# Transposing attention probabilities four heads at a time, and multiplying by values in 64x64 tiles

## The reference

```
x = x + xattn(layernorm(x), ctx_1024, ...)
x = x + ffn(layernorm(x), w_gate, w_up, w_down)

def xattn(x, context, ...):
    q = (layernorm(x) @ w_q).reshape(B, SQ, 16, 64)
    k, v = split(context @ w_kv)                    # 77 keys, 16 heads of 64
    attn = softmax(einsum("bqhd,bkhd->bhqk", q * SCALE, k))
    out = einsum("bhqk,bkhd->bqhd", attn, v).reshape(B, SQ, 1024)
    return (out @ w_out + b_out) * tanh(gate[0])

def ffn(x, w_gate, w_up, w_down):                   # integer weights times 1/127
    return (silu(x @ wg.T) * (x @ wu.T)) @ wd.T
```

## Time and profile before

| | |
|---|---|
| median of 3 runs | 308.63 us |
| the profiled execution | 308.18 us |
| its span, first to last instruction | 305.8 us |
| PE busy | 292.3 us (96%) |
| DVE, ACT, POOL busy | 233.1, 170.4, 165.8 us |
| granted TensorE clock, mean | 0.998 |

### The profile page before, as it was taken

One profiled execution on the slowest core, in us unless ns is written; L12 is line 12 of the kernel. 1 busy time (PEld: TensorE's weight loads), 2 busy tenths in 40 slices (PEclk: granted clock), 3 DMA queues, 4 the chain that ended last, 5 costly groups with the idle time before them and its releaser, 6 DMA issues.

```text
span 305.8 us, 6324 instructions
## 1 busy us (share of the span) xinstructions
PE 292.3 (96%) x2351; PEld 269.6 (88%) x2351; DVE 233.1 (76%) x610; ACT 170.4 (56%) x326; POOL 165.8 (54%) x164
## 2 busy tenths in 40 slices
PE   6899999997989999999999999999999999999985
PEld 6898978786888899889998989898989898988984
DVE  2298897686789788878887797779777878786773
ACT  4456884667328734772496249525943694167052
POOL 3381863357857680857095629553863487227033
PEclk9999999999999999999999999999999999999999
DMA  7994154412423021002201020202020201110001
GB/s 203 376 368 115 38 172 180 173 62 103 147 74 102 0 78 58 13 13 67 69 2 47 31 69 2 76 2 69 3 77 2 69 2 41 34 38 0 2 30 40
DMA packets 16313, 23.27 MB, mean 76 GB/s; under 512 B 1634, under 2 KB 13898, under 8 KB 16282
## 3 DMA queue, kind: packets, MB, share of 16 engines
q1 hardware_dynamic: 16282, 22.85, 22.8%
HBM read 15.87 MB, written 4.62 MB: 67 GB/s over the span
## 4 chain that ended last, share of the span: by engine, by line
PE 86%; DVE 5%; POOL 3%; ACT 2%; issue 2%; DMA 1%; DVEq 0%; POOLq 0%; ACTq 0%; SPq 0%
PE ps L822 13%; PE ps L768 9%; PE ps L754 8%; PE ps L728 6%; PE ps L736 5%; PE ps L732 5%; PE ps L891 5%; PE ps L895 5%; PE ps L892 5%; PE ps L657 5%; PE ps L875 3%; PE ps L878 3%; PE ps L843 2%; PE ps L665 2%; PE ps L667 2%
## 5 line engine op out<-in xcount | busy, mean ns | idle before, releaser
L1124 POOL TENSOR_TENSOR probs<-probs,total 128x616 f32<-128x616 f32 x32 | 39.0, 1218 | 73.8 <-DVE total L1252 73.8
L986 ACT COPY pt<-ps 77x512 f32<-77x512 f32 x64 | 34.1, 583 | 47.2 <-PE ps L754 47.2
L1142 POOL TENSOR_TENSOR h_lo<-hid,h_hi 128x256 fp32r<-128x256 f32 x42 | 30.9, 737 | 32.9 <-ACT h_hi L1053 32.9
L1131 POOL TENSOR_TENSOR t_lo<-t_all,t_hi 128x1232 fp32r<-128x1232 f32 x16 | 45.6, 2848 | 4.7 <-ACT t_hi L1011 4.7
L891 PE MATMUL ps<-wo_hi,o_hi 128*128 128x256 f32 x128 | 36.4, 284 | 0.0
L892 PE MATMUL ps<-wo_lo,o_hi 128*128 128x256 f32 x128 | 36.1, 282 | 0.0
L895 PE MATMUL ps<-wo_hi,o_lo 128*128 128x256 f32 x128 | 35.9, 281 | 0.0
L754 PE MATMUL ps<-ident,probs 128*77 128x128 f32 x256 | 33.2, 273 | 2.1 <-POOL probs L1124 1.8
L1235 DVE TENSOR_REDUCE top<-ps 128x4 f32<-128x308 f32 x64 | 28.7, 472 | 8.3 <-PE ps L736 8.1
L754 PEld LDWEIGHTS ps<-ident,probs 128*77 128x77 f32 x256 | 29.6, 147 | 2.8 <-POOL probs L1124 2.0
L768 PE MATMUL ps<-pt,v 77*64 77x256 f32 x256 | 31.2, 385 | 0.0
(11 more groups left out here) (152 smaller groups left out, 795.4 us busy)
## 6 DMA issues: line engine op xcount, KB each, us to landing
v<-v_scratch SPq DMA_DIRECT2D x8, 308.0 KB
x_ln<-in_x SPq DMA_DIRECT2D x8, 256.0 KB, 3.9
v_scratch<-v_out SPq DMA_DIRECT2D x4, 512.0 KB, 2.9
stream<-in_x SPq DMA_DIRECT2D x8, 256.0 KB, 2.7
x_rooms<-in_x SPq DMA_DIRECT2D x7, 256.0 KB, 8.0
out<-stream SPq DMA_DIRECT2D x7, 256.0 KB, 2.2
wk_raw<-in_L_xattn_w_kv SPq DMA_DIRECT2D x4, 256.0 KB, 4.9
wq_raw<-in_L_xattn_w_q SPq DMA_DIRECT2D x1, 1024.0 KB, 7.8
```

The source lines that it names most:

```text
L986: nc.scalar.copy(pt[:, q * HB:(q + 1) * HB, t * P:(t + 1) * P], ps_p[0:K, m % 2, :].rearrange("k (h q) -> k h q", h=HB)).then_inc(pt_copie ...
L1124: nc.gpsimd.tensor_tensor(p, p, total[:, u, :].unsqueeze(2).to_broadcast([P, HG, K]), ALU.mult).then_inc(probs_done, 1)
L1131: nc.gpsimd.tensor_tensor(t_lo[:, :, cols], t_all[:, :, n, cols], t_hi[:, :, cols].bitcast(F32), ALU.subtract).then_inc(tlo_done, 1)
```

## The change

The 77 keys of a head are cut into 64 ("whole") and 13 ("rest"). In probs two heads, 2j and 2j+1, lie side by side in 154 columns. The middle 128 of these are keys 13 to 76 of the even head and keys 0 to 63 of the odd head, and one transpose of 128 x 128 now turns them together. The four pairs take four transposes, all into bank 4. The 13 columns that are left at either end of each pair are multiplied by POOL into a separate tile `rest` (128 x 128 with zeros between; two such tiles in turn), and a fifth transpose turns that one into bank 5.

So pt holds on partitions 0 to 63 the whole keys of even heads, on 64 to 127 those of odd heads, and in a fifth column block the rest of all. Values are laid out alike: v_whole with 64 keys for each half of the partitions, v_rest with 4 x 13 keys of four heads in each half and zeros elsewhere. A head's product is now two matmuls that accumulate: 64 rows x 64 columns, and 52 rows x 64 columns. Even heads (r = 0) write bank 4, odd ones (r = 1) bank 5. This changes which head lies where in o_hi, so w_out is loaded in the matching order.

A group's banks are handed on once, after the last matmul of V, where before the first bank was handed on halfway. On SP the load of v becomes ten transfers (two of 64 rows, eight of 13 rows, in runs of 256 bytes), the load of w_out eight. In the start, four of these eight come after the second load of x, and two each behind the first and the second store of v; the last four transfers of the first v load come behind the fourth store. POOL gets two fills with zeros in the start.

```diff
-POOL_START = "XS F0 F1 F2 Ta X Tb P0 P1".split()
+POOL_START = "XS F0 F1 F2 VZ Ta X Tb RZ P0 P1".split()
...
+KEYS_WHOLE = 64
...
+    HALVES = 2
+    HR = HG // HALVES
+    NEW = K - KEYS_WHOLE
+    ROOMS = 2
+    NEXT = HALVES * K
...
+    V_LOADS = HALVES + HG
...
-        v = sb("v", [K, INNER])
+        v_whole = sb("v_whole", [P, 2, HR * DH])
+        v_rest = sb("v_rest", [P, 2, HR * DH])
...
-        pt = sb("pt", [K, HG, Q])
+        pt = sb("pt", [P, HR + 1, Q])
+        rest = sb("rest", [P, ROOMS, P])
...
-            def load_v(n):
+            def load_v_whole(n):
...
-                wait(sp, pv_done, NU * n)
-                sp.dma_start(v[:], v_scratch.rearrange("(b k) n -> b k n", k=K)[n]).then_inc(v_in, 16)
+                if isinstance(n, int) and n == 0:
+                    sp.wait_ge(v_zeroed, 1)
+                wait(sp, pv_done, 2 * n)
+                v_rows = v_scratch.rearrange("(b k) n -> b k n", k=K)[n]
+                whole_keys = (slice(NEW, K), slice(0, KEYS_WHOLE))
+                for r in range(HALVES):
+                    half = slice(r * KEYS_WHOLE, (r + 1) * KEYS_WHOLE)
+                    sp.dma_start(v_whole[half].rearrange("k g (j d) -> k (g j) d", d=DH),
+                                 v_rows[whole_keys[r]].rearrange("k (h r d) -> k r h d", r=HALVES, d=DH)[:, r]).then_inc(v_in, 16)
+
+            def load_v_rest(n, r):
...
+                for j in range(HR):
+                    first = r * KEYS_WHOLE + j * NEW
+                    sp.dma_start(v_rest[first:first + NEW, :, j * DH:(j + 1) * DH], by_head[rest_keys[r], r, j]).then_inc(v_in, 16)
...
-                for q in range(2):
-                    m = 2 * t + q
...
-                    for h in range(HB):
-                        hh = q * HB + h
-                        ins = nc.tensor.transpose(ps_p[0:K, m % 2, h * P:(h + 1) * P],
-                                                  probs[:, u, hh * K:(hh + 1) * K], ident[:])
-                    ins.then_inc(pt_done, 1)
+                if t == 0:
+                    wait(pe, olo_done, NU * b + 2 * g)
+                else:
+                    pe.wait_ge(pt_copied, NU * b + u)
+                for j in range(HR):
+                    ins = nc.tensor.transpose(ps_p[:, 0, j * P:(j + 1) * P], probs[:, u, j * NEXT + NEW:j * NEXT + NEW + P], ident[:])
+                ins.then_inc(pt_done, 1)
+                pe.wait_ge(rest_done, NU * b + u + 1)
+                nc.tensor.transpose(ps_p[:, 1, t * P:(t + 1) * P], rest[:, (NU * b + u) % ROOMS, :], ident[:]).then_inc(pt_rest_done, 1)
...
-                for i in range(2):
-                    for pair in range(2):
+                for pair in range(2):
+                    for keys in (v_whole, v_rest):
                         for e in range(2):
-                            h = 4 * i + 2 * pair + e
-                            gh = g * HG + h
-                            ins = mm(ps_p[e * DH:(e + 1) * DH, i, pair * Q:(pair + 1) * Q],
-                                     v[:, gh * DH:(gh + 1) * DH], pt[:, h, :], start=True, stop=True)
-                    ins.then_inc(pv_done, 1)
+                            j = 2 * pair + e
+                            at = j if keys is v_whole else HR
+                            for r in range(HALVES):
+                                half = slice(r * KEYS_WHOLE, r * KEYS_WHOLE + (KEYS_WHOLE if keys is v_whole else HR * NEW))
+                                ins = mm(ps_p[e * DH:(e + 1) * DH, r, pair * Q:(pair + 1) * Q],
+                                         keys[half, g, j * DH:(j + 1) * DH], pt[half, at, :],
+                                         start=keys is v_whole, stop=keys is v_rest)
+                ins.then_inc(pv_done, 1)
...
-                    nc.scalar.copy(pt[:, q * HB:(q + 1) * HB, t * P:(t + 1) * P],
-                                   ps_p[0:K, m % 2, :].rearrange("k (h q) -> k h q", h=HB)).then_inc(pt_copied, 1)
+                nc.scalar.copy(pt[:, 0:HR, t * P:(t + 1) * P],
+                               ps_p[:, 0, :].rearrange("k (j q) -> k j q", j=HR)).then_inc(pt_copied, 1)
+                if t == NT - 1:
+                    act.wait_ge(pt_rest_done, NU * b + u + 1)
+                    nc.scalar.copy(pt[:, HR, :], ps_p[:, 1, 0:Q]).then_inc(pt_rest_copied, 1)
...
             def copy_o(b, g):
+                act.wait_ge(pv_done, 2 * b + g + 1)
                 for i in range(2):
                     n = 2 * g + i
-                    act.wait_ge(pv_done, NU * b + n + 1)
...
             def normalise(b, u):
                 pool.wait_ge(rec_done, NU * b + u + 1)
...
+                nc.gpsimd.tensor_tensor(whole, whole, scale.to_broadcast([P, HR, HALVES, KEYS_WHOLE]),
                                         ALU.mult).then_inc(probs_done, 1)
...
+                wait(pool, pt_rest_done, n + 1 - ROOMS)
...
+                nc.gpsimd.tensor_tensor(to.rearrange("p r (j k) -> p r j k", k=NEW), ends,
+                                        scale.to_broadcast([P, HR, HALVES, NEW]), ALU.mult).then_inc(rest_done, 1)
```

More of the change, by code:

```diff
@@ L109, in xattn_ffn_kernel @@
     X_STEPS = 4 + 12
+    HALVES = 2
[3 more added lines that the diff above has]
+    NEXT = HALVES * K
+    assert KEYS_WHOLE + NEW == K
+    V_LOADS = HALVES + HG
+    assert HALVES * KEYS_WHOLE == P and 0 < HR * NEW <= KEYS_WHOLE
     assert HB * K <= BANK and DC == 2 and NT == 2 and 2 * DH == P and RC == VS + 1 and K <= P
@@ L249, in xattn_ffn_kernel @@
         xln_in, xres_in, v_in, y_out = sem("xln_in"), sem("xres_in"), sem("v_in"), sem("y_out")
-        scores_done, pt_done, pv_done = sem("scores_done"), sem("pt_done"), sem("pv_done")
+        scores_done, pv_done = sem("scores_done"), sem("pv_done")
+        pt_done, pt_rest_done = sem("pt_done"), sem("pt_rest_done")
+        v_zeroed, rest_zeroed = sem("v_rest_zeroed"), sem("rest_zeroed")
         xt_done, x2t_done, gu_done = sem("xt_done"), sem("x2t_done"), sem("gu_done")
@@ L586, in _, with load_wo @@
             sp.wait_ge(s_job, last_t + 1)
-            sp.dma_start(wo_raw[:], w_out.rearrange("(i p) n -> p i n", p=P)).then_inc(s_in["wo"], 16)
+            out_rows = w_out.rearrange("(g n e r d) m -> e g r d n m", g=2, e=2, r=HALVES, d=DH)
+            def load_wo(*which):
+                for i in which:
+                    for e in range(2):
+                        sp.dma_start(wo_raw[e * DH:(e + 1) * DH, 2 * i:2 * i + 2, :],
+                                     out_rows[e, i // HALVES, i % HALVES]).then_inc(s_in["wo"], 16)
             load_ln(1)
+            load_wo(0, 1)
             for r in range(RC):
@@ L593, in _ @@
                              v_out[0:rows(r), v_slot(r), :]).then_inc(s_vrow[r], 16)
+                if r < 2:
+                    load_wo(2 + r)
                 if r == 1:
                     sp.wait_ge(s_vrow[0], 16)
-                    load_v(0)
+                    load_v_whole(0)
+                    load_v_rest(0, 0)
+                if r == 3:
+                    load_v_rest(0, 1)
             stages = {"RES": ("now", load_res), "LN": ("next", lambda n: load_ln(n + 1)), "WD": ("first", weights_in_place, 2),
@@ L976, in copy_pt @@
             def copy_pt(b, g, t):
[L977 to L985, removed]
-                    nc.scalar.copy(pt[:, q * HB:(q + 1) * HB, t * P:(t + 1) * P],
-                                   ps_p[0:K, m % 2, :].rearrange("k (h q) -> k h q", h=HB)).then_inc(pt_copied, 1)
+                u = NT * g + t
+                act.wait_ge(pt_done, NU * b + u + 1)
+                if t == 0:
+                    wait(act, pv_done, 2 * b + g)
+                    if isinstance(b, int) and b == 0 and g == 0:
+                        for row in range(RC):
+                            if v_slot(row) < 2:
+                                act.wait_ge(s_vrow[row], 16)
+                nc.scalar.copy(pt[:, 0:HR, t * P:(t + 1) * P],
[3 more added lines that the diff above has]
+                    nc.scalar.copy(pt[:, HR, :], ps_p[:, 1, 0:Q]).then_inc(pt_rest_copied, 1)
             def copy_o(b, g):
+                act.wait_ge(pv_done, 2 * b + g + 1)
                 for i in range(2):
                     n = 2 * g + i
-                    act.wait_ge(pv_done, NU * b + n + 1)
                     if n == 0:
@@ L1159, in _ @@
             stages["WO"] = ("first", wout_lo)
+            stages["VZ"], stages["RZ"] = ("start", zero_rest), ("start", zero_ends)
             for i in range(3):
```

47 lines of the change are left out of this document (35 added, 12 removed).

## The result

The changed kernel takes 306.12 us (median of 19 runs, 303.78 to 308.5); the kernel before, run beside it, 308.73 us (19 runs, 307.99 to 310.58). The ratio is 0.9898, 95% interval 0.9878 to 0.9917. The medians lie 2.6 us apart; by the ratio it is 3.1 us. The forecast was 301 us, 7.4 less by its sum. The measured time lies inside the range of 8 in 10, which ended at 307.5, but the gain is less than half of the forecast one. The profiled execution took 307.07 us, its span is 305.3 us, the mean granted clock 0.989.

What follows compares the result with a forecast made beforehand. PE, busy 292.3 of 305.8 us, was taken as the bound. Transposes' -10.5 us and losses of 1.3, 0.1, 0.65, 0.25, 0.5, 0.2 and 0.1 gave -7.4 from 308.18: 300.8, as median 301; 8-in-10 range 297.5 to 307.5.

Steps and rivals of the forecast that it cites:

- The prize: On PE, each of 32 units drops from 8 to 5 transposes, taking 10.5 us off.
- the four quadrants: In V, two row halves and two column halves run side by side, so 32 records take 1.74 us, no change.
- rival (a): In V, quadrants don't run four wide; V costs 27.9 us more in all, 328 us, slower; 16% in all.
- Nothing else is taken off PE: On PE, the 10.5 us from fewer transposes is the whole gain.
- Zero for all: Transfers: SP's extra issues at 0.31 us each, small runs and POOL's fills stay hidden, costing zero.
- rival (c): At V0, the values come late through ten issues and small runs; near 310 us; 3%.
- T3's wait: T3 waits for P3, 0.1 us in each of five middle rounds (0.5) and 0.25 in the second.
- the places of loss: Gain lost in the first round (1.31 us), second round (0.65 us) and last round (0.2 us).
- 1.31 us: First round: what T0 to T3 save is lost because wo_lo on POOL comes when it came; 0.1 added.
- X1T of the second round: It waits for LN1 on DVE, about 1.7 us instead of 1.05, so 0.65 us is lost.
- T0 of the last round to the end of the span: Last round: 0.2 us lost to DVE's split of O after V1, at most 0.1 to copies.

Runs made afterwards that it cites:

- experiment 4: The kernel before with five transposes a unit instead of eight, three heads left out, all else as before; 300.96 us, ratio 0.9731.
- experiment 11: Experiment 5 with V's matmuls reordered, all even heads first, then all odd heads; 315.99 us (one run).
- experiment 5: The changed kernel with 46 more matmuls in PE's branch not taken, moving the taken branch by 184 instructions; 303.81 us, ratio 0.9783 to the kernel before.
- experiment 6: The kernel before with 18 more matmuls (72 instructions) in the branch not taken, placing the taken branch as in the change; 311.82 us, ratio 1.0061.
- experiment 12: The changed kernel with 58 more matmuls in the branch not taken, so the taken branch's first block ends after 47 instructions; 303.31 us, ratio 0.9812.
- experiment 1: The changed kernel run again, unaltered, for a second profile; 305.49 us, ratio 0.9879 to the kernel before.
- experiment 2: The changed kernel with the start's transfers in another order on SP; 305.03 us, ratio 0.9835 to the kernel before.
- experiment 8: Experiment 7 with the start's transfers in the other order; 305.23 us, ratio 0.985 to the kernel before.
- experiment 10: Experiment 9 with the start's transfers in the other order; 301.53 us, ratio 0.9737 to the kernel before.
- experiment 3: The kernel before with only the start's transfers cut up as in the change; 309.94 us, ratio 0.9998.
- experiment 9: Experiment 5 with ACT's work on x cut in two, in the order xn, tanh of G0, xn_hi; 300.95 us, ratio 0.9736 to the kernel before.
- experiment 7: Experiment 5 with ACT's tanh of G0 moved ahead of the work on x; 306.61 us, ratio 0.9896 to the kernel before.

## Why the prediction was wrong

**The prize and the four quadrants were right.** -10.5 us for the transposes: experiment 4, which keeps all else, gains 8.3 us by its ratio (0.0269 x 309), where 8 was expected of it, and that with a pause of 0.96 us of its own. V stayed at 1.9 us, and experiment 11 shows that this comes from row halves at work together, rival (a)'s question. The Trainium skill ("TensorE: Matmul & The Clock Gate", Part 3: Packing small matmuls) lets matmuls start and end only in program order; the trace of experiment 11, with its two groups of eight, disagrees for the starts of matmuls of different row halves. The Trainium skill ("TensorEngine Tiling (Array Packing)", Key Properties) has tiles operate independently, and with that the trace agrees.

**The step that failed is a term that the sum did not have.** "Nothing else is taken off PE" was true of the work and silent on PE's own instructions. The sum priced a longer V only by its time in the array; the same 16 matmuls a call, also in the copy of the rounds that is never run, moved the start of the copy that is. Experiments 5, 6 and 12 show that this place alone is worth 3 to 3.5 us in the change and 1.9 in the kernel before: the pause, and in the change a stretch or two at the lower clock. In the change's first profile the first round takes 32.02 us from T0 to T0, in experiment 5's 27.21. What brings the stretches is only in part shown: in the change's profile and those of experiments 1 and 2 one begins 0.06 to 1.22 us behind the pause's end, but the clock stayed up behind experiment 6's pause, and experiment 12 has a stretch far from its own. The rule was to be had: the Trainium skill ("Runtime: NRT & Kernel Launch", Instruction fetch mechanics) says that instructions are refilled in blocks of 16 KiB, the next fetched while one executes, and that a taken branch breaks this prefetch. The traces agree, and add that what the target's block still holds sets the price.

**Mis-sized: the start's transfers, "Zero for all".** In the change an issue of 13 rows takes 0.86 us on SP, not 0.31, and stores lay behind it. The wait that follows is real (1.10 us of PE's time in the change's trace, of which 0.54 to 0.60 stay as "issue" where the order is changed, experiments 8 and 10), but experiments 3 and 10 bound its worth at 0 to 1 us. In the middle rounds eight such issues take 6.64 us and stay hidden, as forecast; rival (c) didn't come.

**Wrong in place and mis-sized: T3's wait.** I gave 0.75 us for P3 in the rounds from the second on. P3 was in time; G3 waited for H0 instead, by the same cause, the O copies that begin after the whole of V. Experiments 5 and 9 size it: 1.52 us between the second round's T0 and the last's (173.14 and 171.62), twice the 0.75 of the sum. With the place's 3 to 3.5 us and the change's own 3.1 by its ratio, this 0.8 makes 6.9 to 7.4, about the forecast.

**Right: the places of loss.** From T0 to the next T0 the first round takes 27.21 us in experiment 5 and 27.30 before, so nothing of 1.31 us is left, as forecast. X1T of the second round waits 1.7 us, as forecast. From T0 of the last round to the end of the span the change takes 40.2 us, 1.15 less than before (forecast 1.0).

The sum of the traces: start 1.45 late, first round 4.7 late (forecast 0.1), rounds 5.6 gained (forecast 6.5), end 1.15 gained, together 0.6 of span. Of the 1.45, 0.74 were there when SP issued the second load of x (41.60 us against 40.86), before any transfer that was changed, and 0.68 already when POOL began the third part of wk_lo (11.82 against 11.14), which the change doesn't touch. In experiment 6, which up to the branch is the kernel before, that part begins at 12.34 and T0 at 60.06 instead of 58.66. T0 starts between 59.35 and 60.34 in experiments 5 and 9, which run the same up to there. So a start that is 1.4 us late needs no change at all, and one trace of each kernel can't tell how much of the 1.45 belongs to this one.

That the change's own runs spread over 4.7 us follows largely from the clock. The three with a mean granted clock of 1.000 took 303.78 to 304.50 us; the nine at 0.993 and 0.994, 304.74 to 307.27; the six at 0.989, 306.74 to 307.57; the one at 0.983, 308.5. One stretch of 3.41 us at half clock takes 0.006 off the mean (3.41 x 0.5 / 305), so these are none, one, two and three stretches. What decides on a stretch stays open. So does what decides, in some executions of several kernels, on a stretch of lower clock near 288 us (0.57 from 288 to 292 us in experiment 5's, none in experiment 9's).

## What to carry to other kernels

When an edit changes how many instructions stand in front of a branch that is taken, its time holds an accident of placement: look for idle "issue" time soon behind the branch, and compare versions only after moving the target so that its first block is long. When a stage hands over its banks later, follow what stands behind the reader on its engine up to the next claim of any bank; moving one step ahead may just exchange the wait (experiment 7), and cutting a step where it frees the bank may free both (experiment 9). Price small transfers by a row of their own shape.

## What the runs showed of the hardware

- A taken branch cost PE 1.77 to 2.30 us when its target's block held 23 instructions more, 0.96 with 31, 0.34 with 47, nothing with 95 (a weight load and a matmul are one each). PE went on 1.20 to 1.46 us after the end of a 16 KB packet of instructions.
- The lower clock came in stretches of 3.41 us: behind PE's pauses of 2.00, 2.18 and 2.30 us, not behind that of 1.77 (experiment 6); behind T3's wait of 1.86 us in the change and of 1.87 in experiment 12, not behind the same wait in experiments 5 and 9.
- fp32 matmuls of 64 x 64 in four quadrants: 32 records of 256 columns in 1.90 us; with the row halves apart 2.81 us, and one half's matmuls overtake the other's.
- Issue on SP by shape: 0.86 us for 13 rows of two runs of 256 bytes, 0.64 for 64 rows, 0.31 for 77 rows of 4 KB.
